# Transposing each own tile once, and scaling the copy by a row of ratios

## The chip, the cores and the metric

One core of a Trainium2 chip runs the whole program. TensorE (matrix products and transposes), VectorE, ScalarE and GpSimd compute, each working through its own list of instructions in order; SyncE issues the transfers. The engines wait for each other through semaphores. The metric is the device time of one execution in microseconds (us); lower is better.

## The reference

The input `x` is 8 sequences of 1024 tokens with 512 channels. Everything is float32.

```python
xn = layernorm(x, eps=1e-5)
out = x + attn(xn) + ffn(xn)
# attn: xs = xn shifted by one token
xm = xn * time_mix + xs * (1 - time_mix)
k = exp(min(xm @ Wk.T, 60)); v = xm @ Wv.T; r = xm @ Wr.T
# per head, a decaying running sum over the tokens
wkv, sum_k = decay_sum(k * v), decay_sum(k)
attn = (sigmoid(r) * wkv / sum_k) @ Wo.T
# ffn: a second layernorm (eps 1e-3), then a ternary product
y = layernorm(xn, eps=1e-3) * ln_gamma + ln_beta
g = max(abs(y)) over the whole input
ffn = clip(y * 128 / g) @ w_ternary * (g * beta / 128)
```

Both layernorms take mean and variance of the same token, so the second result is the first one times a number of that token. `g` is a maximum over all eight sequences, so no product of the second part can begin before all of `y` is known.

## The kernel before, in words

**Phases.** The eight sequences are worked off as batches 0 to 7, each in two tiles of 512 tokens (t = 0, 1). Phase A is batches 0 to 3: the attention part of the batch, and besides the second layernorm of that batch ("own") and of the batch four later ("other"), whose results go to memory while VectorE keeps their largest absolute value. Phase B is batches 4 to 7: the attention part again, and the ternary products of all eight batches.

**A batch** is 24 groups (g = 0 to 23). Group g is `project(g)` on TensorE, 12 products of 128x128 by 512 columns (float32 split into a high and a low part, three products for each of four channel blocks): k, v and r in turn for one 128-channel chunk c = g // 3. Chunks 0 to 3 belong to tile 0, chunks 4 to 7 to tile 1. After group 12 comes `attn_out` of tile 0, after group 23 that of tile 1: 48 products each, four chunks j by four banks by three. Chunk j is multiplied when VectorE has made its low part (`rwkv_lo`, L996); behind that stands a long chain on VectorE and ScalarE for every chunk: exp, k*v (L966), two scans (L976), a sum (L983), logarithm (L731), quotient (L736), product (L992), high part (L750) and low part.

**Slots.** In phase A each group also carries one slot: four transposes of 128x128 (L466) that bring one channel block of a normalised tile into a PSUM bank with the channels on the partitions. The order of the 24 slots is written out by hand: `ffn_own0` (slots 0 to 3), `ffn_other0` (4 to 7), `mix_own1` (8 to 11), `ffn_own1` (12 to 15), `ffn_other1` (16 to 19), `mix_next0` (20 to 23; the next batch's tile 0). Two banks take turns. ScalarE empties a slot (`evacuate`): a mix slot by two instructions (L616, L617) from which VectorE makes the mixed input (L898), ScalarE its high part (L662) and VectorE its low part (L922); an ffn slot by one (L625, scale gamma, bias beta), an "other" one by two (L624 keeps a plain copy). VectorE then takes the absolute maximum of an ffn slot (L905). TensorE's group 12 needs the four low parts of `mix_own1`, the next batch's group 0 those of `mix_next0`.

**Where the slots' tiles come from.** An own tile is normalised twice into the same buffer `normed`, once for the mix slots and once for the ffn slots: two of its four 128-token blocks by GpSimd (L1174), two by ScalarE (L677). The second waits until the transposes of the first have read the buffer. The scales are made on GpSimd by small instructions, after VectorE's statistics (L842; in groups 4, 12, 16 and at the batch's end).

**The start.** TensorE transposes four mix slots of batch 0 (`"P"`), while the weights are split into high parts (ScalarE for Wk and Wr, GpSimd for Wv and Wo) and low parts (VectorE, L927). ScalarE goes on to batch 0 when the low parts of Wr are done.

**Phase B** has no slots. The mix input is read back from memory, and GpSimd multiplies it by a row (L1247).

Of the kernel before, what the change touches and what calls it, by code (L numbers as in the profile page):

```python
# [22 lines left out]
F32 = mybir.dt.float32  # L23
# [5 lines left out]
P = 128  # L29
# [27 lines left out]

BANK_USES = {"A": ["attn0", "attn1"],
# [4 lines left out]
def mixed_decay_kernel(nc, x, constants, weights, Wf, out):  # L63
# [19 lines left out]
    with ExitStack() as ctx:  # L83
# [27 lines left out]
        AL = sb("ffn_lo", [P, CH, TILE], F32R)  # L111
        KV = sb("k_and_kv", [P, 2, 2, TILE])
# [18 lines left out]
        inv = sb("mix_over_ffn_stat", [P, 2, Q])  # L131
        gamb = sb("gamma_beta", [P, CH])
# [47 lines left out]
        act_c = sem("act_constants")  # L180

# [21 lines left out]
        pool_v = sem("pool_mix_input")  # L203

# [8 lines left out]
        STEPS, MIX_STEPS, OTHER_STEPS = 9, 3, 3  # L213
# [5 lines left out]
        def slots_before(b, ph, n):  # L219

            return n if ph == "P" else CH + len(SLOTS) * b + n

# [26 lines left out]
        def normed_count(b, ph, kind):  # L249

            if ph == "A":
                return 4 * b + [k for k in SLOT_KINDS if "other" not in k].index(kind) + 1
            return 4 * HALF + 2 * (b - HALF) + ["mix_own1", "mix_next0"].index(kind) + 1
# [36 lines left out]
        first_banks = [TB[:, :]] + [KVR[:, i, :] for i in range(3)]  # L290
# [16 lines left out]
        def _(sp):  # L307
# [35 lines left out]
            def batch_a(b, is_last=False):  # L343
                for n in range(7):
                    store_ffn_input(b, n)
                sp.wait_ge(pe_t, slots_before(b, "A", first_slot("ffn_other0") + CH))
# [12 lines left out]
                if not is_last:  # L359
                    sp.wait_ge(pe_t, slots_before(b, "A", first_slot("ffn_other1") + CH))  # L360
                    sp.dma_start(ZA[:, :, :], x_t[b + HALF + 1, 0]).then_inc(s_oth, 16)
                store_ffn_input(b, 19)
                store_row(b, 1)
                if is_last:
# [7 lines left out]
                    sp.wait_ge(pe_t, slots_before(b, "A", first_slot("ffn_other1") + CH))  # L372
                    for ch in range(CH):
                        sp.dma_start(ZA[:, ch, :], ffn_in[0, 0, ch]).then_inc(s_fld[ch], 16)
                    sp.wait_ge(pe_t, slots_before(b, "A", len(SLOTS)))
# [80 lines left out]
        def _(pe):  # L456
            pe.sem_inc(pe_g, CREDIT)
            pe.sem_inc(pe_rw, BANKS - 1)
# [18 lines left out]
            pe.wait_ge(dve_x, 2)  # L477

            def slot(b, ph, n):
                kind, ch = slot_of(ph, n)  # L480

                pe.wait_ge(act_u, slots_before(b, ph, n) - (n not in (0, ATTN0_AFTER + 1)))
                if n == 1:
                    pe.wait_ge(dve_out, BANKS + bank_use(b, ph, "attn0"))
                if n == ATTN0_AFTER + 2:
# [32 lines left out]
            def attn_out(b, ph, t):  # L518
# [3 lines left out]
                for j in range(CH):  # L522
                    pe.wait_ge(dve_rl, RING + CHUNKS * b + 4 * t + j + 1)
                    for q in range(Q):
                        if j == 0 and ph == "A":
                            pe.wait_ge(dve_out, first_bank + q + 1)
                            if q == Q - 1:
# [62 lines left out]
        def _(act):  # L590
# [3 lines left out]

            def evacuate(b, ph, n):
# [5 lines left out]
                if ph != "B":  # L601
                    act.wait_ge(pe_t, m + 1)
# [11 lines left out]
                elif mix:  # L614
                    if ph != "P":
                        nc.scalar.activation(U[:, r, :], bank, ACT.Copy, scale=tmx[:, ch:ch + 1])  # L616
                    nc.scalar.activation(shifted(ph, n), bank, ACT.Copy,  # L617
                                         scale=tmx1[:, ch:ch + 1]).then_inc(act_u, 1)
                elif ph == "A":
# [5 lines left out]
                    nc.scalar.activation(U[:, r, :], bank, ACT.Identity, bias=bet[:, ch:ch + 1],  # L625
# [38 lines left out]
            def normalise(b, ph, kind):  # L664
# [9 lines left out]
                i = 4 * b if kind == "ffn_own0" else stats_number(b, ph, tile)  # L674
                act.wait_ge(pool_step, STEPS + steps_before(i, ph) + (OTHER_STEPS if "other" in kind else STEPS if ffn else MIX_STEPS))
# [32 lines left out]
            act.wait_ge(pool_step, STEPS + STEPS)  # L708
            for q in ACT_CHUNKS:
                last = nc.scalar.activation(XN[:, q, :], X[0][:, q, :], ACT.Identity,  # L710
                                            bias=own[:, 0, 3, q:q + 1], scale=own[:, 0, 2, q:q + 1])
            last.then_inc(act_xn, 1)
            weight_hi("r")

# [583 lines left out]
```

## Time and profile before

| | |
|---|---|
| median of 3 runs | 892.61 us (891.09 to 892.99) |
| the profiled execution, its own time | 891.49 us |
| its span, first to last instruction | 889.7 us |
| TensorE busy (products) | 867.1 us, 97% of the span |
| VectorE | 764.8 us, 86% |
| ScalarE | 510.3 us, 57% |
| GpSimd | 215.2 us, 24% |
| granted clock of TensorE over the span | 1.000 |

In the profile PE is TensorE, PEld its weight loads, DVE VectorE, ACT ScalarE, POOL GpSimd; L12 is line 12 of the kernel. A timeline row reads: start and length in us, engine, line, operation, output<-input with partitions x elements, how many were merged, and in brackets the idle time before it and what ended it. TensorE's products are pipelined, so starts are compared, not lengths. In the view of busy time in stretches each row reads: the stretch, its length, then busy us (and instructions) of PE, PEld, DVE, ACT and POOL, the granted clock of TensorE, the share of time that the DMA engines worked, and GB/s. Batch 1 runs from 125.60 to 224.50.

### The profile page before, as it was taken

Reading aid. Unit: us, or ns where it says so; the run is one execution under the profiler, and the core shown is the slowest. Engines: PE = TensorE matmul, PEld = TensorE weight load, DVE = VectorE, ACT = ScalarE, POOL = GpSimd, SP = SyncE. Lnnn points to the kernel's source line nnn. Section 1 sums busy time; section 2 is a strip of 40 time slices with the busy share of each in tenths; the row PEclk is TensorE's granted clock in tenths of the full one; section 3 lists DMA queues with packets and bytes.
Section 4 is the critical chain, followed back from the end, with each engine's and each line's share of the span. In section 5 each row is a group of like instructions: output and inputs, shape, how many; then the busy total and the mean of one; then the engine's idle time right before and its main releaser. Section 6 shows DMA issues by size and latency. Waiting matters only on the chain.

```text
span 889.7 us, 12792 instructions
## 1 busy us (share of the span) xinstructions
PE 867.1 (97%) x3984; PEld 714.5 (80%) x3984; DVE 764.8 (86%) x1278; ACT 510.3 (57%) x834; POOL 215.2 (24%) x242
## 2 busy tenths in 40 slices
PE   3989999999999999999999999999999999999998
PEld 2778888888888888888888888888888888888886
DVE  5998999989897999989897897878978888789684
ACT  5584767667594757566564554545546536365441
POOL 5552326242452425240030100200201103011000
PEclk9999999999999999999999999999999999999999
DMA  8222415041423224045643245324451443424311
GB/s 283 108 83 88 149 54 184 13 171 54 165 71 135 101 82 154 12 172 136 212 145 115 84 154 189 125 75 141 153 175 57 157 141 96 154 93 142 95 48 47
DMA packets 59841, 107.13 MB, mean 120 GB/s; under 512 B 7712, under 2 KB 7712, under 8 KB 59808
## 3 DMA queue, kind: packets, MB, share of 16 engines
q1 hardware_dynamic: 59808, 106.73, 35.1%
q8 instruction: 16, 0.26, 0.1%
q14 instruction: 17, 0.14, 0.1%
HBM read 64.76 MB, written 41.96 MB: 120 GB/s over the span
## 4 chain that ended last, share of the span: by engine, by line
PE 90%; DVE 3%; issue 2%; POOL 2%; ACT 1%; DMA 0%; SPq 0%; POOLq 0%; DVEq 0%; ACTq 0%
PE kvr L513 18%; PE kvr L515 18%; PE kvr L514 18%; PE out_banks L552 7%; PE out_banks L554 7%; PE out_banks L534 6%; PE out_banks L533 6%; PE out_banks L531 6%; PE transposed L466 2%; PE out_banks L466 2%; DVE bn_stats L842 1%; POOL normed L1174 1%; POOL own_stats L1156 1%; POOL own_stats L1157 1%; DMA x<-in_x 0%
## 5 line engine op out<-in xcount | busy, mean ns | idle before, releaser
L1247 POOL TENSOR_TENSOR evacuated<-normed,mix_over_ffn_row 128x512 f32<-128x512 f32 x28 | 49.0, 1751 | 339.0 <-DVE ffn_lo L922 339.0
L513 PE MATMUL kvr<-xm_hi,wk_hi 128*128 128x512 f32 x256 | 103.7, 405 | 2.6 <-DVE xm_lo L922 2.6
L513 PE MATMUL kvr<-xm_hi,wv_hi 128*128 128x512 f32 x256 | 102.9, 402 | 2.2 <-DVE wv_lo L927 1.3
L513 PE MATMUL kvr<-xm_hi,wr_hi 128*128 128x512 f32 x256 | 102.7, 401 | 0.0
L515 PE MATMUL kvr<-xm_hi,wk_lo 128*128 128x512 f32 x256 | 101.0, 395 | 0.0
L514 PE MATMUL kvr<-xm_lo,wk_hi 128*128 128x512 f32 x256 | 100.7, 394 | 0.0
L515 PE MATMUL kvr<-xm_hi,wv_lo 128*128 128x512 f32 x256 | 100.2, 391 | 0.0
L515 PE MATMUL kvr<-xm_hi,wr_lo 128*128 128x512 f32 x256 | 100.1, 391 | 0.0
L531 PE MATMUL out_banks<-wo_hi,rwkv_hi 128*128 128x512 f32 x256 | 100.0, 390 | 0.0
L534 PE MATMUL out_banks<-wo_hi,rwkv_lo 128*128 128x512 f32 x256 | 99.7, 389 | 0.0
L514 PE MATMUL kvr<-xm_lo,wr_hi 128*128 128x512 f32 x256 | 99.7, 389 | 0.0
L514 PE MATMUL kvr<-xm_lo,wv_hi 128*128 128x512 f32 x256 | 99.7, 389 | 0.0
L552 PE MATMUL out_banks<-w_ternary,ffn_hi 128*128 128x512 f32 x256 | 99.6, 389 | 0.0
L533 PE MATMUL out_banks<-wo_lo,rwkv_hi 128*128 128x512 f32 x256 | 99.6, 389 | 0.0
L554 PE MATMUL out_banks<-w_ternary,ffn_lo 128*128 128x512 f32 x256 | 99.6, 389 | 0.0
L724 ACT ACTIVATE gate<-kvr 128x512 f32<-128x512 f32 x64 | 37.9, 593 | 90.7 <-PE kvr L515 90.7
L983 DVE SCALAR_TENSOR_TENSOR k_and_kv<-k_and_kv,constants,scans 128x1024 f32<-128x1024 f32 x64 | 83.3, 1302 | 1.1
L976 DVE TENSOR_TENSOR_SCAN scans<-constants,state,k_and_kv 128x512 f32<-128x512 f32 x64 | 79.7, 1286 | 0.0
L976 DVE TENSOR_TENSOR_SCAN scans<-constants,k_and_kv 128x512 f32<-128x512 f32 x64 | 75.8, 1226 | 0.0
L662 ACT ACTIVATE ffn_hi<-evacuated 128x512 fp32r<-128x512 f32 x64 | 39.9, 624 | 48.5 <-DVE evacuated L908 46.2
L1174 POOL TENSOR_SCALAR normed<-x,own_stats 128x512 f32<-128x512 f32 x34 | 55.0, 1623 | 51.2 <-PE out_banks L466 26.1
L922 DVE TENSOR_TENSOR ffn_lo<-evacuated,ffn_hi 128x512 fp32r<-128x512 f32 x64 | 43.9, 687 | 25.4 <-ACT ffn_hi L662 25.1
(140 smaller groups left out, 1922.7 us busy)
## 6 DMA issues: line engine op xcount, KB each, us to landing
other<-ffn_input SPq DMA_DIRECT2D x64, 256.0 KB, 5.1
x<-in_x SPq DMA_DIRECT2D x15, 1024.0 KB, 5.8
other<-in_x SPq DMA_DIRECT2D x8, 1024.0 KB, 5.8
ffn_input<-evacuated SPq DMA_DIRECT2D x32, 256.0 KB, 4.4
ffn_input<-parked SPq DMA_DIRECT2D x32, 256.0 KB, 2.2
attn_scratch<-x SPq DMA_DIRECT2D x8, 1024.0 KB, 4.2
parked<-attn_scratch SPq DMA_DIRECT2D x8, 1024.0 KB, 6.7
out<-parked SPq DMA_DIRECT2D x8, 1024.0 KB, 5.2
```

Of the source, the lines that this page charges most:

```text
L513: nc.tensor.matmul(KVR[:, m, :], hi, XH[t][:, ch, :], start=(ch == 0), stop=False)
L514: nc.tensor.matmul(KVR[:, m, :], hi, XL[t][:, ch, :], start=False, stop=False)
L515: last = nc.tensor.matmul(KVR[:, m, :], lo, XH[t][:, ch, :], start=False, stop=(ch == CH - 1))
L531: nc.tensor.matmul(OUT[:, q, :], hi, WH["o"][:, j, :], start=(j == 0 and ph == "A"), stop=False)
L533: nc.tensor.matmul(OUT[:, q, :], hi, WL["o"][:, j, :], start=False, stop=False)
L534: last = nc.tensor.matmul(OUT[:, q, :], lo, WH["o"][:, j, :], start=False, stop=(j == CH - 1))
L552: nc.tensor.matmul(OUT[:, q, :], AH[:, ch, q * P:(q + 1) * P], WQ[:, ch, :], start=(ch == 0), stop=False)
L554: last = nc.tensor.matmul(OUT[:, q, :], AL[:, ch, q * P:(q + 1) * P], WQ[:, ch, :], start=False, stop=(not own_tile and ch == CH - 1))
L976: last = V.tensor_tensor_scan(S[:, i, 1:TILE + 1], dec, kv[:, i, :], 0.0 if t == 0 else state[:, j, i:i + 1], ALU.mult, ALU.add)
L983: V.scalar_tensor_tensor(kv, kv, first[:, j:j + 1], S[:, :, 0:TILE], ALU.mult, ALU.add).then_inc(dve_sum, 1)
L1174: last = G.tensor_scalar(dst[:, q, :], src[:, q, :], stats[:, 2 * ffn, q:q + 1], stats[:, 2 * ffn + 1, q:q + 1], ALU.mult, ALU.add)
L1247: G.tensor_tensor(U[:, n % RING, :], XN[:, ch, :], BC[:, :], ALU.mult).then_inc(pool_v, 1)
```

## The change

An own tile is normalised once, for the mix slots. While ScalarE empties a mix slot it also copies the plain transposed block into a new buffer `Y`. The second layernorm of the same block is that copy times a row with one ratio for each token, `(var / (var + 1e-5) + 1e-3) ** -0.5`. GpSimd makes the ratios as columns (its last small steps fall away), TensorE turns each column, repeated 128 times, into a row that stands on all partitions (four transposes for a tile, into an output bank, after groups 9 and 21; the very first into the bank of the slots), ScalarE copies the row to SBUF, and GpSimd multiplies `Y` by it, one instruction of 128x512 for each block. The ffn slots of own tiles become virtual: ScalarE empties them from `Y` and TensorE has nothing to do for them. The "other" tiles and phase B stay as they are.

```diff
+        def is_virtual(n):
+            return SLOTS[n][0].startswith("ffn_own")
...
+ROW_AFTER = {9: 1, 21: 0}
...
     # TensorE
+            def ratio_row(k, t, bank):
+                pe.wait_ge(pool_ratio, k + 1)
+                for q in range(Q):
+                    last = nc.tensor.transpose(bank[:, q * P:(q + 1) * P],
+                                               ratio[:, t, q:q + 1].to_broadcast([P, P]), ident[:, :])
+                last.then_inc(pe_row, 1)
+
+            ratio_row(0, 0, TB)
...
-                    if ph == "B":
+                    if ph == "B" or n is not None and is_virtual(n):
                         n = None
...
+                    if ph == "A" and g in ROW_AFTER:
+                        t = ROW_AFTER[g]
+                        pe.wait_ge(dve_out, bank_use(b, ph, f"attn{1 - t}") + 1)
+                        ratio_row(2 * b + 2 - t, t, OUT[:, 0, :])
...
     # ScalarE
+            def copy_row(k, t, bank):
+                act.wait_ge(pe_row, 2 + k + 1)
+                nc.scalar.activation(RROW[:, t, :], bank, ACT.Copy).then_inc(act_row, 1)
...
+                if virtual:
+                    act.wait_ge(pool_z, virtual_before(b, n) + 1)
...
+                        nc.scalar.activation(Y[:, ch, :], bank, ACT.Copy)
                         nc.scalar.activation(U[:, r, :], bank, ACT.Copy, scale=tmx[:, ch:ch + 1])
...
-                    nc.scalar.activation(U[:, r, :], bank, ACT.Identity, bias=bet[:, ch:ch + 1],
+                    nc.scalar.activation(U[:, r, :], Y[:, ch, :] if virtual else bank, ACT.Identity,
...
+                    if ph == "A" and g - 1 in ROW_AFTER:
+                        t = ROW_AFTER[g - 1]
+                        copy_row(2 * b + 2 - t, t, OUT[:, 0, :])
                     if part1_first:
                         evacuate(b, ph, n)
...
-                                normalise(b, ph, "ffn_own1")
...
-                    normalise(b + 1, ph, "ffn_own0")
...
     # ScalarE in the start, after the high parts of Wr
+            for ch in range(CH):
+                last = nc.scalar.activation(Y[:, ch, :], first_banks[ch], ACT.Copy)
+            copy_row(0, 0, TB[:, :])
...
     # GpSimd
-                pool.wait_ge(pe_t, slots_before(b, "A", first_slot("mix_own1") + CH))
-                normalise(XN, X[1], own[:, 1], 1, pool_xn)
+                for ch in range(CH):
+                    own_ffn_input(b, first_slot("ffn_own1") + ch)
                 other(b, "other1")
...
-                    normalise(XN, X[0], own[:, 0], 1, pool_xn)
+                    for ch in range(CH):
+                        own_ffn_input(b + 1, first_slot("ffn_own0") + ch)
                     other(b + 1, "other0")
+
+            def own_ffn_input(b, n):
+                kind, ch = SLOTS[n]
+                t = int(kind[-1])
+                pool.wait_ge(act_row, 2 * b + t + 1)
...
+                G.tensor_tensor(Y[:, ch, :], Y[:, ch, :], RROW[:, t, :], ALU.mult).then_inc(pool_z, 1)
```

In the start GpSimd's four multiplies for batch 0 stand between its casts of Wo and its work on the first "other" tile. TensorE's waits for free slot banks are counted over the slots that are left.

## Rows read from the trace of the kernel before

**Rows 1.** Busy time in two stretches: a batch of phase A, one of B.

```profile
125.60:224.50 98.90, 98.80 (x482) 81.37 (x481) 90.39 (x159) 66.28 (x108) 39.24 (x48) 1.00 0.31 107
...
530.00:649.00 119.00, 119.00 (x526) 98.54 (x525) 99.06 (x157) 60.04 (x98) 14.64 (x8) 1.00 0.38 128
```

**Rows 2.** The same view: groups 0 to 3 and 8 to 11, batch 1.

```profile
125.60:138.40 12.80, 12.80 (x66) 10.56 (x65) 11.54 (x23) 6.22 (x9) 7.30 (x9) 1.00 0.63 224
...
151.30:164.30 13.00, 13.00 (x65) 10.84 (x66) 12.86 (x25) 11.66 (x21) 5.55 (x8) 1.00 0.23 81
```

**Rows 3.** Timeline of TensorE: slots 9 and 10 of batch 1.

```profile
154.54 0.60 PE L466 MATMUL out_banks<-ident,normed 128*128 128x128 f32 x4
...
157.74 0.60 PE L466 MATMUL transposed<-ident,normed 128*128 128x128 f32 x4
```

**Rows 4.** The same in phase B: first products of two groups in a row.

```profile
427.48 0.39 PE L513 MATMUL kvr<-xm_hi,wr_hi 128*128 128x512 f32 x1
...
430.19 0.39 PE L513 MATMUL kvr<-xm_hi,wk_hi 128*128 128x512 f32 x1
```

**Rows 5.** Timeline of all engines: slot 8 of batch 1.

```profile
148.28 2.95 POOL L1174 TENSOR_SCALAR normed<-x,own_stats 128x512 f32<-128x512 f32 x2 [0.39 <-POOL own_stats L1157]
...
151.29 0.66 PE L466 MATMUL transposed<-ident,normed 128*128 128x128 f32 x4
```

**Rows 6.** Timeline of ScalarE in batch 1.

```profile
139.55 0.59 ACT L624 ACTIVATE parked<-transposed 128x512 f32<-128x512 f32 x1
140.03 0.78 ACT L625 ACTIVATE evacuated<-transposed,constants 128x512 f32<-128x512 f32 x1
...
163.92 0.64 ACT L662 ACTIVATE xm_hi<-evacuated 128x512 fp32r<-128x512 f32 x1
...
216.35 0.72 ACT L731 ACTIVATE k_and_kv<-k_and_kv,k_eps 128x512 f32<-128x512 f32 x1 [0.93 <-DVE k_and_kv L983]
```

**Rows 7.** Timeline of VectorE in batch 1.

```profile
161.21 1.29 DVE L922 TENSOR_TENSOR xm_lo<-evacuated,xm_hi 128x512 fp32r<-128x512 f32 x2
...
163.72 1.71 DVE L922 TENSOR_TENSOR xm_lo<-evacuated,xm_hi 128x512 fp32r<-128x512 f32 x2
...
173.89 0.69 DVE L996 TENSOR_TENSOR rwkv_lo<-k_and_kv,rwkv_hi 128x512 fp32r<-128x512 f32 x1 [0.70 <-ACT rwkv_hi L750]
...
219.89 0.69 DVE L996 TENSOR_TENSOR rwkv_lo<-k_and_kv,rwkv_hi 128x512 fp32r<-128x512 f32 x1
```

**Rows 8.** Timeline of TensorE: end of group 12, last chunks of both outputs.

```profile
166.17 0.39 PE L513 MATMUL kvr<-xm_hi,wk_hi 128*128 128x512 f32 x1
...
175.49 0.39 PE L531 MATMUL out_banks<-wo_hi,rwkv_hi 128*128 128x512 f32 x1
...
221.57 0.39 PE L531 MATMUL out_banks<-wo_hi,rwkv_hi 128*128 128x512 f32 x1
```

**Rows 9.** View of line 1247: min/median/max in ns, first and last start.

```profile
L1247 POOL TENSOR_TENSOR evacuated<-normed,mix_over_ffn_row x28: 1288/1297/3455, 446.9 to 808.5; 128x512 f32<-128x512 f32 x28
```

**Rows 10.** Timeline of all engines in phase B around one GpSimd multiply.

```profile
517.14 0.74 DVE L890 SCALAR_TENSOR_TENSOR evacuated<-evacuated,constants,shifted_part 128x511 f32<-128x511 f32 x1
...
518.56 1.30 POOL L1247 TENSOR_TENSOR evacuated<-normed,mix_over_ffn_row 128x512 f32<-128x512 f32 x1 [7.03 <-DVE ffn_lo L922]
...
518.59 1.82 DVE L890 SCALAR_TENSOR_TENSOR evacuated<-evacuated,constants,shifted_part 128x511 f32<-128x511 f32 x1
```

**Rows 11.** Timeline of VectorE in the start.

```profile
21.91 4.15 DVE L927 TENSOR_TENSOR wv_lo<-x,wv_hi 128x512 fp32r<-128x512 f32 x4
...
25.98 2.48 DVE L927 TENSOR_TENSOR wr_lo<-k_and_kv,wr_hi 128x512 fp32r<-128x512 f32 x4
...
35.20 0.67 DVE L966 TENSOR_TENSOR k_and_kv<-k_and_kv,kvr 128x512 f32<-128x512 f32 x1
```

**Rows 12.** Waits of TensorE: total us, times, longest; first and last.

```profile
PE transposed L466 <- POOL normed L1174: 14.3, 2, 12.1
...
PE kvr L513 <- DVE k_and_kv L966: 0.9, 1, 0.9
```

More of the change, by code:

```diff
@@ L56 @@
 RING = 4
+FFN_ROOM = 176640
+ROW_AFTER = {9: 1, 21: 0}
 BANK_USES = {"A": ["attn0", "attn1"],
@@ L180, in mixed_decay_kernel @@
         act_c = sem("act_constants")
+        act_first = sem("act_first_own_copied")
+        act_row = sem("act_ratio_row_copied")
+        pe_row = sem("pe_ratio_row")
         dve_c = sem("dve_constants")
@@ L203, in mixed_decay_kernel @@
         pool_v = sem("pool_mix_input")
+        pool_ratio = sem("pool_ratio_row")
+        pool_z = sem("pool_own_ffn_input")
         dve_past = sem("dve_past_wait")
@@ L221, in slots_before, with pe_slots_before, virtual_before @@
             return n if ph == "P" else CH + len(SLOTS) * b + n
+        def is_virtual(n):
+            return SLOTS[n][0].startswith("ffn_own")
+        def pe_slots_before(b, ph, n):
+            if ph == "P":
+                return n
+            per_batch = sum(not is_virtual(k) for k in range(len(SLOTS)))
+            return CH + per_batch * b + sum(not is_virtual(k) for k in range(n))
+        def virtual_before(b, n):
+            return 2 * CH * b + sum(is_virtual(k) for k in range(n))
         def ffn_stores_before(b, n):
@@ L251, in normed_count @@
             if ph == "A":
-                return 4 * b + [k for k in SLOT_KINDS if "other" not in k].index(kind) + 1
-            return 4 * HALF + 2 * (b - HALF) + ["mix_own1", "mix_next0"].index(kind) + 1
+                return 2 * b + ["mix_own1", "mix_next0"].index(kind) + 1
+            return 2 * HALF
         def stats_number(b, ph, tile):
@@ L288, in shifted @@
             return E[:, n % 2, :] if ph == "P" and n > 1 else WS[:, n % 2, :]
-        first_banks = [TB[:, :]] + [KVR[:, i, :] for i in range(3)]
+        first_banks = [OUT[:, q, :] for q in range(Q)]
         def slot_bank(ph, n):
@@ L457, in _ @@
             pe.sem_inc(pe_g, CREDIT)
+            pe.sem_inc(pe_row, 2)
             pe.sem_inc(pe_rw, BANKS - 1)
@@ L526, in attn_out @@
                             pe.wait_ge(dve_out, first_bank + q + 1)
+                            if q == 0:
+                                pe.wait_ge(act_row, 2 * b + 2 + t)
                             if q == Q - 1:
@@ L600, in evacuate @@
                 mix = kind.startswith("mix")
-                if ph != "B":
-                    act.wait_ge(pe_t, m + 1)
+                virtual = ph == "A" and is_virtual(n)
+                if virtual:
+                    act.wait_ge(pool_z, virtual_before(b, n) + 1)
+                elif ph != "B":
+                    act.wait_ge(pe_t, pe_slots_before(b, ph, n) + 1)
                 act.wait_ge(dve_lo, m + 1)
@@ L672, in normalise @@
                 ffn = kind.startswith("ffn")
-                i = 4 * b if kind == "ffn_own0" else stats_number(b, ph, tile)
-                act.wait_ge(pool_step, STEPS + steps_before(i, ph) + (OTHER_STEPS if "other" in kind else STEPS if ffn else MIX_STEPS))
+                i = stats_number(b, ph, tile)
+                act.wait_ge(pool_step, STEPS + steps_before(i, ph) + (OTHER_STEPS if "other" in kind else MIX_STEPS))
                 for q in ACT_CHUNKS:
@@ L707, in _ @@
                 high_part(0, "P", m)
[L708 to L712, printed above, removed]
             weight_hi("r")
+            for ch in range(CH):
+                last = nc.scalar.activation(Y[:, ch, :], first_banks[ch], ACT.Copy)
+            last.then_inc(act_first, 1)
+            copy_row(0, 0, TB[:, :])
             act.wait_ge(dve_w, 3 * CH)
@@ L1005, in add_out @@
                     for normed in (pool_xn, act_xn):
-                        dve.wait_ge(normed, CREDIT + (4 * HALF if ph == "B" else normed_count(b, ph, f"ffn_own{t}")))
+                        dve.wait_ge(normed, CREDIT + (2 * HALF if ph == "B" else 2 * b + t))
                     if ph == "B":
@@ L1181, in _ @@
             normalise(XN, X[0], own[:, 0], 0, pool_xn)
-            ffn_scale(0, 0, own[:, 0])
-            pool.wait_ge(pe_t, CH)
-            normalise(XN, X[0], own[:, 0], 1, pool_xn)
+            ffn_scale(0, 0, own[:, 0], 0, 0)
             pool.wait_ge(s_w[1], 16)
@@ L1252, in batch_b @@
                         mix_input(b, n)
+            for ch in range(CH):
+                own_ffn_input(0, first_slot("ffn_own0") + ch)
             other(0, "other0")
```

47 lines of the change are left out of this document (26 added, 21 removed).

## The prediction

> **What bounds the kernel now.** I read the busy time in stretches first, to see which engine sets each stage [rows 1]. In a batch of phase A (125.60 to 224.50) TensorE is busy 98.80 of 98.90 us, in a batch of phase B 119.00 of 119.00: TensorE sets the time, and the list of its waits [rows 12] is short: the longest entry is 14.3 us, 12.1 of them the wait for the first normalised tile. So a transpose taken off TensorE is worth its time, as long as nobody else becomes late. The second view is who is next. VectorE is busy 90.39 us of that batch, but not evenly: over groups 8 to 11 it has 12.86 of 13.00 us, and ScalarE 11.66 of 13.00 [rows 2], while in groups 0 to 3 VectorE has 1.26 us free and ScalarE 6.58. The third view is the timeline around the points where TensorE reads what VectorE wrote last; there I read margins.
>
> **What is removed, and what a slot is worth.** Two neighbouring slots of the mix tile start 3.20 us apart (157.74 - 154.54) with the twelve matmuls of one group between them [rows 3]. In phase B the same twelve without a slot take 2.71 us (430.19 - 427.48) [rows 4]. A slot of four transposes costs TensorE 0.49 us. Per batch eight slots go and two rows of four transposes come. A row's transposes have the same shape as a slot's, but read one column repeated, which no row shows; bounds are nothing (a load of repeated values could be cheaper) and twice a slot, 0.98. I take 0.49, since the form and the output are those of rows 3. So TensorE gains 8 x 0.49 - 2 x 0.49 = 2.94 us a batch. In batch 0 slots 0 to 3 are worth nothing: TensorE there waits in any case for VectorE's k*v of chunk 0 (0.9 us [rows 12], ending at 35.87 [rows 11]) and would only wait longer. Batch 0 gains 0.98. The ceiling is 3 x 2.94 + 0.98 = 9.8 us. The ninth row lies in the start, where TensorE has idle time.
>
> **Does the gain of groups 0 to 3 survive to group 8?** Slot 8 was started by GpSimd's normalise (148.28 + 2.95 = 151.23, TensorE at 151.29 [rows 5]), so that chain had no margin. Its head is the statistics behind slot 4, and slot 4 comes as much earlier as four slots are worth; VectorE has 1.26 us free in groups 0 to 3 and what it waits for there is TensorE's. I let the whole 1.96 through. The steps that the new row needs are small ones of four columns right behind that normalise, and the row stands two groups later, 6.4 us by rows 3: no wait.
>
> **Place 1, groups 8 to 13.** ScalarE gets four copies of the mix tile and a row copy ahead of the high part of slot 11. A copy from PSUM occupies it 0.48 us (140.03 - 139.55 [rows 6]): 2.4 us. It had 1.34 us free there [rows 2]; I let it absorb 1.0, as part of its idle time is too early. The high part moves from 163.92 to about 165.3 (bounds: 1.06 and 2.4 late). The last low part then ends near 166.6 instead of 163.72 + 1.71 = 165.43 [rows 6, 7]. TensorE wants it at 166.17 [rows 8], 0.49 later because of the row: just met. But behind it VectorE has the whole recurrence of chunk 3, and its rwkv_lo ended at 173.89 + 0.69 = 174.58 against TensorE's 175.49 [rows 7, 8]: margin 0.91, less 1.2: 0.3 us of stall. (The removed normalise of ScalarE stood behind the high part, so it gives nothing back to this chain; the row and the missing slot 12 cancel on TensorE.)
>
> To this come GpSimd's four multiplies, 1.30 us each where undisturbed (median of 28, up to 3.46) [rows 9], which must pass VectorE in its fullest stretch. Rows 10 show the price of a collision: the same instruction of 511 columns takes 0.74 us alone and 1.82 beside a multiply, 1.08 more. The two chunks of the normalise that now go cost VectorE 0.42 (1.71 against 1.29 for two low parts [rows 7]). Bounds for four multiplies: nothing (all in instructions or gaps that don't mind) and 4 x 1.08 - 0.42 = 3.9 us. I take 1.7: one fits where VectorE now waits for ScalarE, one in k*v from PSUM or the absmax, two collide. Stall at place 1: 0.3 + 1.7 = 2.0 us a batch (0.3 to 4.2).
>
> The Trainium skill ("SBUF — State Buffer", "Who interferes with whom") has the rule against this change: a VectorE instruction with two SBUF inputs and a GpSimd instruction that reads SBUF exclude each other for a whole instruction. The trace agrees in kind: 1.08 of 1.30 us [rows 10]. By the rule's full 1.30 the same share of collisions would cost, as an estimate, 0.22 us more each, some four a batch: 3.5 us more than my sum in all.
>
> **Place 2, groups 20 to 23 and the second output.** Three ScalarE copies (the row, two of the mix tile; those for slots 20 and 21 fall into its idle time) add 1.44 us ahead of the logarithm of chunk 7, which had waited 0.93 [rows 6]: 0.5 late. VectorE's last rwkv_lo ended at 219.89 + 0.69 = 220.58, TensorE reads at 221.57 [rows 7, 8]; with the row's 0.49 the margin is 1.48, less 0.5: 1.0. Four multiplies again, of which I let two collide (2.2) less the normalise taken away (0.42): 1.7 - 1.0 = 0.7 us (0 to 2.9). They must be done by the next batch's slot 0, over 10 us later: no wait.
>
> **The start.** ScalarE's copies and the row copy follow the casts of Wr, so the four multiplies become possible at about 25.7, when VectorE begins its four low parts of Wr (2.48 us [rows 11]). Four casts of GpSimd beside the low parts of Wv cost VectorE 4.15 - 2.48 = 1.67 us [rows 11]; four multiplies cost between nothing and 4 x 1.08 = 4.3. I take 2.5, the 1.67 drawn out by the longer instruction. All that VectorE does up to k*v of chunk 0 moves with it, and TensorE waits for that: + 2.5 us.
>
> **The sum.** Batches 1 to 3: 3 x (-2.94 + 2.0 + 0.7) = -0.7. Batch 0: -0.98 + 2.7 = +1.7. Start +2.5. Together +3.5 us, slower. The profiled execution took 891.49 us (span 889.7 and 1.8 around it), so 895.0 by its own time; it lies 1.1 below the median of the three runs, 892.61, and against that I predict 896.0. Nothing else moves: phase B, SyncE's order of transfers and the VectorE work per slot are the same.
>
> **Rivals.** With s for the stall of a batch, the change is 2.5 + 4s - 9.8.
> 1. *Slower, as summed* (s = 2.7): VectorE, already full in groups 8 to 13, is pushed by ScalarE and GpSimd past TensorE. For it: 0.14 us free in 13.00 [rows 2], margins under 1 us. From s = 2.3 it is over 0.2% slower. 896.
> 2. *Faster*: GpSimd's multiplies wait until VectorE does statistics, absmax or sums out of PSUM, and cost it nothing; only ScalarE's lateness stays. s = 0.5 and 1.0 at the start: 1.0 + 2.0 - 9.8 = -6.8, 886. It decides for s below about 1.4. For it: two normalise chunks in the fullest stretch cost VectorE only 0.42 [rows 7], and the median multiply ran undisturbed [rows 9]. Against: the multiply holds on longer, and rows 10.
> 3. *Break-even*: s between 1.4 and 2.3, within 1.8 us (0.2%, about what a measurement can tell from no change). 893.
> 4. *A new wait*: the first multiply of a tile is starved; ScalarE's evacuation of slot 12 stands ahead of exp, logarithm and quotient of chunks 3 and 4, so all of them wait. The longest multiply was 3.46 us, 2.2 over the median [rows 9]; once a batch on top of place 1: +8.6 on the sum, 905. Against: ScalarE reaches that slot two groups after the row copy. The Trainium skill ("SBUF — State Buffer", the same section) lets the instruction issued first go first; a VectorE that is back to back would then keep GpSimd out, which is this case. No row of phase A has a multiply.
> 5. *The row costs twice a slot*: 8 x 0.49 = +3.9 on any of these; I see no sign of it and count it inside their spread.
>
> **How the numbers follow.** Chances: slower as summed 0.42, faster 0.31, break-even 0.20, new wait 0.07. So faster 0.31, same 0.20, slower 0.49. The extreme ends of the bounds (s = 0.3 with no cost at the start, -8.6; s = 7.1 with 4.3, +23) are unlikely to meet. The range leaves out a tenth on each side: 886 to 904; the likeliest case's own is 894.5 to 902.
>
> **What the profile afterwards would show.** Right: 32 multiplies of 128x512 on GpSimd in phase A, 92 fewer transposes (128 out, 36 in); a pitch between batches of 98 to 100 us; TensorE idle ahead of the first product of group 12 or of the output product, released by low parts or rwkv_lo, 1 to 3 us a batch; VectorE instructions of two SBUF inputs lengthened by about 1 us beside multiplies; k*v of chunk 0 near 38. Wrong: a batch pitch near 96 with no such idle time (rival 2), or ScalarE waiting for GpSimd at slot 12 (rival 4).

## The result, and the profile after

The change takes 917.61 us (median of 4, 916.51 to 917.84) against 892.43 us (median of 4, 891.09 to 892.99): ratio 1.0282, 95% interval 1.0264 to 1.0300. It is slower, as forecast, but by 25 us where 3.5 were forecast, far outside the range of 886 to 904. The profiled execution has a span of 914.2 us against 889.7. The prediction named a pitch between batches of 98 to 100 us as its sign; batch 1 now takes 104.8 us, 98.9 before.

The page first: busy time of each engine, and the engines' shares of the chain that ended last.

```profile
PE 867.5 (95%) x3892; PEld 709.4 (78%) x3892; DVE 791.5 (87%) x1278; ACT 521.3 (57%) x863; POOL 242.8 (27%) x246
...
PE 60%; DVE 19%; issue 10%; ACT 4%; POOL 3%; DMA 3%; DVEq 0%; ACTq 0%; SPq 0%; POOLq 0%
```

VectorE has as many instructions as before (1278) and is busy 26.7 us longer (791.5 against 764.8). So it has no more work; its instructions have become longer. TensorE's list of waits, which answers to [rows 12]:

```profile
PE kvr L556 <- DVE xm_lo L979: 12.3, 11, 2.0
PE out_banks L576 <- DVE rwkv_lo L1053: 6.4, 3, 2.1
PE kvr L556 <- DVE wr_lo L984: 3.7, 1, 3.7
```

These three lie at the three places of the prediction: place 1 (group 12; 2.6 of the 12.3 us belong to the start, as before), place 2 (the second output) and the start. Timelines of place 1 in batch 1, GpSimd, VectorE, then TensorE, to be held against [rows 7, 8]:

```profile
169.45 7.14 POOL L1306 TENSOR_TENSOR own_normed<-own_normed,ffn_over_mix_rows 128x512 f32<-128x512 f32 x4 [5.43 <-ACT ffn_over_mix_rows L647]
...
171.97 3.49 DVE L979 TENSOR_TENSOR xm_lo<-evacuated,xm_hi 128x512 fp32r<-128x512 f32 x2
175.38 1.76 DVE L1049 TENSOR_TENSOR k_and_kv<-k_and_kv,gate 128x512 f32<-128x512 f32 x1
...
178.47 0.50 PE L556 MATMUL kvr<-xm_hi,wk_hi 128*128 128x512 f32 x1 [1.99 <-DVE xm_lo L979]
```

Two low parts take 3.49 us instead of 1.29 beside the multiplies, a product 1.76 instead of 0.69: three instructions of VectorE are lengthened by about 1.1 us each at four multiplies. TensorE stands for 1.99 us ahead of the third quarter of group 12. Place 2 in the same batch:

```profile
224.39 6.89 POOL L1306 TENSOR_TENSOR own_normed<-own_normed,ffn_over_mix_rows 128x512 f32<-128x512 f32 x4 [8.56 <-ACT ffn_over_mix_rows L647]
...
216.94 2.45 DVE L1033 TENSOR_TENSOR_SCAN scans<-constants,state,k_and_kv 128x512 f32<-128x512 f32 x2
...
224.39 0.68 DVE L1023 TENSOR_TENSOR k_and_kv<-k_and_kv,kvr 128x512 f32<-128x512 f32 x1
224.98 0.73 DVE L1028 COPY scans<-state 128x2 f32<-128x2 f32 x1
225.63 4.56 DVE L1033 TENSOR_TENSOR_SCAN scans<-constants,state,k_and_kv 128x512 f32<-128x512 f32 x2
230.23 2.13 DVE L1040 SCALAR_TENSOR_TENSOR k_and_kv<-k_and_kv,constants,scans 128x1024 f32<-128x1024 f32 x1
...
234.50 0.50 PE L576 MATMUL out_banks<-wo_hi,rwkv_hi 128*128 128x512 f32 x1 [2.14 <-DVE rwkv_lo L1053]
```

The two scans of the chunk before took 2.45 us (at 216.94, no multiply beside them), here 4.56; the sum takes 2.13 instead of 1.28. Together 2.96 us, again for three of four multiplies: the first lay beside k*v out of PSUM, which took 0.68 us as ever. The copy of 128x2 behind it took 0.73 us instead of 0.16, so 3.5 us in all. The gap of TensorE stands ahead of the third of the output's four chunks. The prediction read its margin ahead of the fourth (0.99 us [rows 7, 8]); ahead of the third it was 217.71 + 0.68 against 218.85 in the kernel before, 0.46 us:

```profile
217.71 0.68 DVE L996 TENSOR_TENSOR rwkv_lo<-k_and_kv,rwkv_hi 128x512 fp32r<-128x512 f32 x1
...
218.85 0.39 PE L531 MATMUL out_banks<-wo_hi,rwkv_hi 128*128 128x512 f32 x1
```

Behind the 2.14 us gap TensorE is slow for a while. Busy time in three stretches, from that gap's end on (columns as in [rows 1], granted clock third from the end):

```profile
234.50:235.50 1.00, 1.00 (x4) 0.86 (x5) 0.96 (x2) 0.24 (x2) 0.00 (x0) 1.00 0.00 0
235.50:238.90 3.40, 3.40 (x9) 2.64 (x8) 3.27 (x8) 1.95 (x4) 0.00 (x0) 0.50 0.00 0
238.90:241.60 2.70, 2.70 (x13) 2.21 (x12) 2.09 (x4) 0.46 (x1) 0.00 (x0) 0.99 0.00 0
```

At 0.50 (1.2 instead of 2.4 GHz) a product takes 0.43 us, not 0.23: 24 products from 234.50 on last 7.19 us to the next group, 1.7 longer than at full clock.

In the start, VectorE's four low parts of Wr stand beside the first four multiplies, and all four are lengthened (2.48 us in [rows 11]):

```profile
25.59 6.81 DVE L984 TENSOR_TENSOR wr_lo<-k_and_kv,wr_hi 128x512 fp32r<-128x512 f32 x4
```

The view of line 1306 has all 32 multiplies (min/median/max in ns, first and last start):

```profile
L1306 POOL TENSOR_TENSOR own_normed<-own_normed,ffn_over_mix_rows x32: 1294/1744/2219, 25.5 to 383.5; 128x512 f32<-128x512 f32 x32
```

One by one in the trace, 7 of them took 1.29 to 1.34 us and 25 took 1.70 to 2.22. The lengthened VectorE instructions of some size are 25 as well: 4 in the start, 12 at place 1, 9 at place 2, by 0.85 to 1.1 us each.

The ledger by groups is worked out from the starts of the first products of each group: pitch after less pitch before, in us, batches 0 to 3. A slot that is gone is worth -0.35 to -0.49 in it.

| kernel | group 12 (place 1) | group 23 (place 2) |
|---|---|---|
| the change | +3.86 +2.63 +3.79 +2.61 | +3.67 +3.69 +2.07 0.00 |
| no multiplies | -0.17 -0.13 -0.14 -0.14 | -0.36 -0.36 -0.35 0.00 |
| `Y` filled, not multiplied | -0.19 -0.17 -0.17 -0.17 | -0.36 -0.37 -0.35 0.00 |
| no copies on ScalarE | +1.92 +3.83 +2.65 +3.61 | +3.69 +2.08 +3.72 0.00 |
| multiplies of place 2 and start moved | +1.85 +3.87 +2.55 +3.81 | -0.35 -0.37 -0.35 -0.01 |
| all multiplies moved | -0.24 -0.19 -0.22 -0.24 | -0.36 -0.36 -0.35 0.00 |

In batch 3 the change itself has no multiplies at place 2 (there is no next batch in phase A), but the row and ScalarE's copy for it: 0.00. At place 1 the batches of the change differ by the clock alone: ahead of the third quarter of group 12 TensorE stands for 1.98 to 2.00 us in all four; the clock falls in 0 and 2 (+3.8) and stays at 1.00 in 1 and 3 (+2.6). But the 1.2 us of that fall are not lost for good. From the first product of group 12 to slot 20, 39.2 to 39.3 us pass in all four batches: those without a fall wait 1.05 us at slot 20 for the next batch's tile, those with one don't.

### The profile page after: what moved, and what is told of

The parts are those of the page before. It is cut to its first block, busy times and chain, and to the rows that moved or that the text cites. A ratio compares the mean times of both kernels' runs of the same rounds, so it can differ in the third digit from the quotient of the medians.

```text
span 914.2 us, 12688 instructions
## 1 busy us (share of the span) xinstructions
PE 867.5 (95%) x3892; PEld 709.4 (78%) x3892; DVE 791.5 (87%) x1278; ACT 521.3 (57%) x863; POOL 242.8 (27%) x246
## 4 chain that ended last, share of the span: by engine, by line
PE 60%; DVE 19%; issue 10%; ACT 4%; POOL 3%; DMA 3%; DVEq 0%; ACTq 0%; SPq 0%; POOLq 0%
PE kvr L556 11%; PE kvr L558 11%; PE kvr L557 11%; PE out_banks L597 6%; PE out_banks L599 6%; PE out_banks L576 5%; PE out_banks L578 5%; PE out_banks L579 5%; DVE scans L1033 4%; DVE bn_stats L899 3%; DVE x L1071 1%; DVE xm_lo L979 1%; DVE k_and_kv L1049 1%; POOL normed L1233 1%; DVE k_and_kv L1023 1%
## 5 line engine op out<-in xcount | busy, mean ns | idle before, releaser
L1316 POOL TENSOR_TENSOR evacuated<-normed,mix_over_ffn_row 128x512 f32<-128x512 f32 x28 | 51.3, 1831 | 336.8 <-DVE ffn_lo L979 336.8
L556 PE MATMUL kvr<-xm_hi,wk_hi 128*128 128x512 f32 x256 | 103.2, 403 | 12.3 <-DVE xm_lo L979 12.3
L576 PE MATMUL out_banks<-wo_hi,rwkv_hi 128*128 128x512 f32 x256 | 102.4, 400 | 6.5 <-DVE rwkv_lo L1053 6.4
L578 PE MATMUL out_banks<-wo_lo,rwkv_hi 128*128 128x512 f32 x256 | 101.7, 397 | 0.0
L1040 DVE SCALAR_TENSOR_TENSOR k_and_kv<-k_and_kv,constants,scans 128x1024 f32<-128x1024 f32 x64 | 85.9, 1342 | 1.1
L1033 DVE TENSOR_TENSOR_SCAN scans<-constants,state,k_and_kv 128x512 f32<-128x512 f32 x64 | 84.8, 1367 | 0.0
L808 ACT ACTIVATE rwkv_hi<-k_and_kv 128x512 fp32r<-128x512 f32 x64 | 40.3, 630 | 55.5 <-DVE k_and_kv L1049 55.5
L556 PEld LDWEIGHTS kvr<-xm_hi,wk_hi 128*128 128x128 f32 x256 | 48.3, 189 | 27.1 <-DVE xm_lo L979 16.0
L1306 POOL TENSOR_TENSOR own_normed<-own_normed,ffn_over_mix_rows 128x512 f32<-128x512 f32 x32 | 55.7, 1771 | 47.7 <-ACT ffn_over_mix_rows L647 47.7
```

Source lines behind the costliest of these rows:

```text
L556: nc.tensor.matmul(KVR[:, m, :], hi, XH[t][:, ch, :], start=(ch == 0), stop=False)
L576: nc.tensor.matmul(OUT[:, q, :], hi, WH["o"][:, j, :], start=(j == 0 and ph == "A"), stop=False)
L578: nc.tensor.matmul(OUT[:, q, :], hi, WL["o"][:, j, :], start=False, stop=False)
L1033: last = V.tensor_tensor_scan(S[:, i, 1:TILE + 1], dec, kv[:, i, :], 0.0 if t == 0 else state[:, j, i:i + 1], ALU.mult, ALU.add)
L1040: V.scalar_tensor_tensor(kv, kv, first[:, j:j + 1], S[:, :, 0:TILE], ALU.mult, ALU.add).then_inc(dve_sum, 1)
L1306: G.tensor_tensor(Y[:, ch, :], Y[:, ch, :], RROW[:, t, :], ALU.mult).then_inc(pool_z, 1)
```

## Experiments

**What blocks VectorE.** First the multiplies were left out, then ScalarE's copies, then each multiply was replaced by a fill of the same block.

```diff
 # no multiplies (GpSimd does nothing to Y; ScalarE waits for its own copy)
-                for ch in range(CH):
-                    own_ffn_input(b, first_slot("ffn_own1") + ch)
...
 # no copies
-                        nc.scalar.activation(Y[:, ch, :], bank, ACT.Copy)
...
 # fills
-                G.tensor_tensor(Y[:, ch, :], Y[:, ch, :], RROW[:, t, :], ALU.mult).then_inc(pool_z, 1)
+                G.memset(Y[:, ch, :], 1.0).then_inc(pool_z, 1)
```

> The multiplies are left out: ScalarE empties the virtual slots from the copy as it is, so the second layernorm lacks its ratio. All else stays, ScalarE's copies and the rows of ratios too. Theory 1 (the multiplies hold up VectorE's instructions of two SBUF inputs, and TensorE waits for VectorE): 884 to 889, that is 3 to 8 us under the kernel before, since the eight slots taken off TensorE then count and only the lateness of ScalarE's copies is left. Theory 2 (ScalarE's copies make the chains late): 905 or more. Theory 3 (the rows of ratios on TensorE and their waits in order): 905 or more.

Measured: 891.68 us, 0.9989 of before (0.9980 to 0.9999). 26 us come back, and both stalls are gone (table). But 884 to 889 was expected: nearly all of TensorE's gain is still missing. That question is taken up below.

> ScalarE's copy of each mix slot into the new buffer is left out (the multiplies work on what is in the buffer); rows and multiplies stay. Theory 1: 912 to 917, little under the changed kernel, for the multiplies are all there. Theory 2: 889 to 895. Theory 3: 913 to 918.

Measured: 915.83 us, 1.0248 (1.0225 to 1.0272). Theory 1 as to the 25 us; theory 2 falls. Theory 3 would give the same time here, but it fell with the kernel without multiplies, which keeps the rows and their waits.

> Each multiply becomes a fill of the same 128x512 block with ones: GpSimd writes SBUF but reads none. Theory 1 in the form that what GpSimd reads is what blocks VectorE: 884 to 890, as without multiplies. Theory 1 in the form that any GpSimd work on SBUF blocks VectorE: in between, 895 to 912, by the length of the fills. Theories 2 and 3: 910 to 918.

Measured: 891.39 us, 0.9988 (0.9978 to 0.9999), as without multiplies. Fills of 0.53 us (median) at the same places cost VectorE 0.1 us in all. Busy time of the engines, without multiplies and with fills:

```profile
PE 860.4 (97%) x3892; PEld 705.6 (79%) x3892; DVE 761.4 (86%) x1278; ACT 520.2 (59%) x863; POOL 189.8 (21%) x214
```

```profile
PE 861.0 (97%) x3892; PEld 706.3 (79%) x3892; DVE 761.5 (86%) x1278; ACT 519.8 (58%) x863; POOL 206.8 (23%) x246
```

VectorE is busy 761.4 and 761.5 us against 791.5 with the change: 30.1 us for 32 multiplies, 0.94 us each, on average over all of them. GpSimd's multiplies take 1771 ns on average, where they take 1300 when nothing is in the way (below): each side waits for the other. They take turns: where they collide VectorE has no pause, and still each multiply comes in after one instruction of VectorE. The Trainium skill ("SBUF — State Buffer", "Who interferes with whom") says that a VectorE instruction with two SBUF inputs contends with a GpSimd instruction that reads SBUF, not with one that only writes it; the trace agrees on both halves.

A fourth kernel let GpSimd read one input, the row, instead of two.

```diff
+                G.tensor_copy(Y[:, ch, :], RROW[:, t, :]).then_inc(pool_z, 1)
```

> Each multiply becomes a copy of the row of ratios into the block: GpSimd reads one input instead of two, for 0.6 to 1.0 us instead of 1.30, at the same places (the second layernorm is replaced by the row). Theory 1, blocked by what GpSimd reads, for as long as it reads: 896 to 908, between no multiplies and the change. If only two inputs on both sides block: 890 to 893, as with the fills.

Measured: 893.23 us, 1.0011 (1.0001 to 1.0021): below the expected range of theory 1 and just above that of its rival. The lines view has the copies at 963 ns on average (607 at the least), and the page has VectorE at 769.2 us:

```profile
L1307 POOL COPY own_normed<-ffn_over_mix_rows 128x512 f32<-128x512 f32 x32 | 30.1, 963 | 64.2 <-ACT ffn_over_mix_rows L647 50.0 <-ACT shifted_part L675 10.7 <-issue 1.9
```

So a reading copy does block, 7.8 / 32 = 0.24 us each, but a microsecond for four of them is within the margins of both places (group 12 -0.06 to -0.02, group 23 -0.34 to 0.00). What was wrong was to scale the time with the blocked time: below the margin it is almost free.

**The same multiplies beside other work.** The next batch's four wait for the last low part of the batch, those of the start for the low parts of Wr.

```diff
+                    pool.wait_ge(dve_lo, RING + slots_before(b, "A", len(SLOTS)))
                     for ch in range(CH):
                         own_ffn_input(b + 1, first_slot("ffn_own0") + ch)
...
+            pool.wait_ge(dve_w, 3 * CH)
             for ch in range(CH):
                 own_ffn_input(0, first_slot("ffn_own0") + ch)
```

> Complete computation. The four multiplies for the next batch's first tile wait until VectorE has made the last low part of the batch, so that they lie beside its sums out of PSUM and its statistics; the four of the start wait for the last low part of Wr. The four of the other tile stay where they are. Theory 1: the stall ahead of the last chunk of the second output goes in batches 0 to 2 (pitch of group 23 3.67, 3.69 and 2.07 longer than before, now within 0.3 of it), so 9 us less, and the start gives 2 us back: 905 to 909. Theories 2 and 3: 914 to 918, unchanged.

Measured: 906.85 us, 1.0143 (1.0126 to 1.0160). Place 2 is clean. The time lies in the expected range with one of its two terms missing, partly by luck: the three stalls at place 2 were 10.5 us (against the kernel without multiplies) where 9 were expected, and the start gave nothing back. Its timeline shows side by side what is blocked and what not:

```profile
28.07 2.46 DVE L899 BATCH_NORM_STATS2 bn_stats<-other 128x6 f32<-128x512 f32 x4
...
30.96 4.67 DVE L984 TENSOR_TENSOR wo_lo<-parked,wo_hi 128x512 fp32r<-128x512 f32 x4
...
28.42 6.06 POOL L1308 TENSOR_TENSOR own_normed<-own_normed,ffn_over_mix_rows 128x512 f32<-128x512 f32 x4 [2.62 <-DVE wr_lo L984]
```

The statistics (one input) take 2.46 us beside the first multiplies, as they take alone; four low parts (two inputs) take 4.67 beside the later ones instead of 2.47.

Then all of them were moved: the other tile's behind the low part of chunk 3, with ScalarE's evacuation and VectorE's maximum of slot 12 behind them, and in the start two behind the low parts of Wr, two behind those of Wo.

```diff
+                pool.wait_ge(dve_rl, RING + CHUNKS * b + CH)
                 for ch in range(CH):
                     own_ffn_input(b, first_slot("ffn_own1") + ch)
```

> Complete computation, all 32 multiplies, each beside work of VectorE that doesn't have two SBUF inputs. Besides what was moved before: the four of the other tile wait for the low part of chunk 3, so that they lie beside the statistics and the sums of the first output (ScalarE's evacuation and VectorE's maximum of slot 12 move behind them); of the four in the start two lie beside the statistics, two wait until the low parts of Wo are made. Theory 1: 891 to 895, what the kernel without multiplies takes, plus 0 to 3 for the start; pitch of group 12 back to within 0.5 of before. A rival within it, that a multiply costs its time wherever it stands (GpSimd and VectorE share more than the second input): 906 to 918, as 32 x 1.0 would still be paid somewhere.

Measured: 896.37 us, 1.0044 (1.0029 to 1.0058). With the same 32 multiplies 21 of the 25 us are gone; the rival that a multiply costs its time anywhere falls. Timelines of GpSimd and VectorE in batch 1, four multiplies beside statistics and sums out of PSUM:

```profile
180.30 5.06 POOL L1316 TENSOR_TENSOR own_normed<-own_normed,ffn_over_mix_rows 128x512 f32<-128x512 f32 x4 [21.83 <-DVE rwkv_lo L1056]
...
179.95 2.46 DVE L902 BATCH_NORM_STATS2 bn_stats<-other 128x6 f32<-128x512 f32 x4
...
182.87 2.48 DVE L1074 TENSOR_TENSOR x<-x,out_banks 128x512 f32<-128x512 f32 x4
```

Neither side is lengthened (1.27 us a multiply). VectorE's busy time is 762.5 us. One of the 32 still collided, in the start, with an instruction that has a single SBUF input; the same takes 0.42 us alone:

```profile
33.30 1.32 DVE L1018 TENSOR_SCALAR k_and_kv<-k_and_kv 128x512 f32<-128x512 f32 x1
```

**Where TensorE's gain goes.** Without multiplies 9.8 us were still to be gained, and 1.0 came. The ledger of that kernel has a loss of 1.1 to 1.4 us in group 19 of every batch (the pitch that holds slot 20) and of 0.4 to 0.5 in group 3 (slot 4) of batches 1 to 3. Its timelines, VectorE, SyncE (SPq is its issue of a transfer) and TensorE in batch 1:

```profile
177.69 2.48 DVE L1074 TENSOR_TENSOR x<-x,out_banks 128x512 f32<-128x512 f32 x4
...
180.20 0.37 SPq L385 DMA_DIRECT2D attn_scratch<-x  x1
...
184.46 0.38 SPq L388 DMA_DIRECT2D x<-in_x  x1
...
190.41 2.47 DVE L902 BATCH_NORM_STATS2 bn_stats<-x 128x6 f32<-128x512 f32 x4 [1.17 <-DMA x<-in_x]
...
199.91 0.66 PE L499 MATMUL out_banks<-ident,normed 128*128 128x128 f32 x4 [0.98 <-POOL normed L1236]
```

The sums of the first output end at 180.17, are stored, the next batch's tile is loaded into the same buffer, and VectorE, idle for it, begins the statistics at 190.41: 10.2 us that don't get shorter when three slots leave groups 13 to 15. In the expectations below, theory 4 is that this way holds TensorE up at slot 20, theory 5 that ScalarE's copies use up the rest of the gain. The first try was to take slot 20 behind the products of group 20, with and without multiplies.

```diff
-                    late = g == ATTN0_AFTER or (is_first and g < 2 * CH)
+                    late = g == ATTN0_AFTER or (is_first and g < 2 * CH) or (ph == "A" and g == 20)
```

> No multiplies (the second layernorm lacks its ratio), and slot 20 behind the products of group 20. Theory 4: 4 to 5 us under the kernel without multiplies, 886 to 888, and no wait of TensorE at slot 20 left. Theory 5: 890 to 893.

Measured: 891.58 us, 0.9983 (0.9973 to 0.9993). The wait at slot 20 is gone (group 19 now -0.35 to -0.44), but group 20 is 0.3 longer and group 23 is +0.74 to +0.91 instead of -0.36: with slot 20 later, TensorE waits 0.6 to 1.0 us for rwkv_lo at the third chunk of the second output. That this comes by way of ScalarE's chain was not tested.

> Complete computation: as the kernel with all multiplies moved, and TensorE takes slot 20 behind the products of group 20 instead of ahead of them. Theory 4 (what the multiplies leave of the gain goes into a wait for the next batch's tile, which comes from memory no earlier than before, 1.2 to 1.4 us at slot 20 in each batch): 4 to 5 us under the kernel with slot 20 in its place, so 886 to 891. Theory 5 (the copies on ScalarE use up the rest): no difference within 1 us.

Measured: 896.38 us, 1.0049 (1.0032 to 1.0065): no difference, theory 4 in this form brings nothing. With all multiplies moved there was little left to gain at slot 20: group 19 loses 0.1 to 0.4 there, because a new wait of 0.9 us at slot 16 stands ahead of it. The second try shortens the way itself, by quarters.

```diff
-                sp.wait_ge(dve_out, BANKS + bank_use(b, "A", "attn0") + Q)
-                sp.dma_start(scratch_t[b, 0], X[0][:, :, :]).then_inc(s_xst[0], 16)
-                store_ffn_input(b, 13)
-                sp.wait_ge(s_xst[0], 16 * b + 16)
-                sp.dma_start(X[0][:, :, :], x_t[b + 1, 0]).then_inc(s_x[0], 16)
+                for q in range(Q):
+                    sp.wait_ge(dve_out, BANKS + bank_use(b, "A", "attn0") + q + 1)
+                    sp.dma_start(scratch_t[b, 0][:, q, :], X[0][:, q, :]).then_inc(s_xsq[q], 16)
+                for q in range(Q):
+                    sp.wait_ge(s_xsq[q], 16 * b + 16)
+                    sp.dma_start(X[0][:, q, :], x_t[b + 1, 0][:, q, :]).then_inc(s_x[0], 16)
+                store_ffn_input(b, 13)
```

> No multiplies (the second layernorm lacks its ratio), and the first tile's way through memory by quarters. Theory 4 in its second form: 886 to 888.5, no wait of TensorE at slot 20. If the wait only moves on: 891 to 892.

Measured: 885.82 us, 0.9924 (0.9911 to 0.9938). The loss in group 19 is gone (-0.06 to 0.00), and 5.0 us with it by the two profiles (5.9 between the medians): theory 4 in its second form.

> No multiplies and no copy of the mix slots on ScalarE either (the second layernorm is made from what is in the buffer). Theory 5 (ScalarE's copies use up what the multiplies leave of the gain): 885 to 889. Theory 4: 891 to 892, as with the copies.

Measured: 886.65 us, 0.9929 (0.9913 to 0.9944), so theory 5 holds as well, at other places: group 19 still loses 0.84 to 1.10, but group 12 is -0.84 to -0.87 instead of -0.13 to -0.17, and group 3 -0.13 in batches 1 and 2 instead of +0.5. ScalarE's copies cost 0.7 us at place 1 and 0.65 at slot 4. Each of the two takes about half of the gain; both edits together weren't tried. The kernel before with the quarters alone is the control:

> The kernel before, with the first tile's way through memory by quarters and nothing else. Theory 4 (the wait for that way appears only when slots 12 to 15 leave TensorE): 892 to 893, no change. If the kernel before waited for it as well: 887 to 889.

Measured: 893.36 us, 1.0008 (0.9997 to 1.0019): it didn't wait for that way.

**A version faster than both.** With all multiplies moved the start still cost 3.5 us up to slot 8 of batch 0 (55.80 against 52.31), and slot 16 had its new wait of 0.9 us. First only GpSimd's order in the start was changed (two multiplies, the normalise of the other tile, two multiplies).

> Complete computation: as the kernel with all multiplies moved, but in the start GpSimd makes two of the four multiplies only after its normalise of the first other tile, for which TensorE waited 2.56 us in that kernel. Theory 1: the 4.3 us that the start still cost shrink to 1 to 2.5: 893 to 895. If the start's loss is not GpSimd's order: 896 again.

Measured: 894.90 us, 1.0024 (1.0014 to 1.0035). With the quarters besides:

> Complete computation: as the kernel with the start mended, and the first tile's way through memory (sums of the first output stored, the next batch's tile loaded into the same buffer) goes by quarters instead of as a whole, ahead of the stores of slots 13 to 15. Theory 4 in its second form (the gain is lost because this way takes 10.0 us, 180.2 to 190.4 in the kernel without multiplies, and TensorE's shorter groups 13 to 15 don't shorten it): the wait at slot 20 goes, 3 to 5 us less: 888 to 892. If it only moves on, as with slot 20 put later: as before this edit within 1 us.

Measured: 892.13 us, 1.0004 (0.9993 to 1.0014): just above the range. Group 19 loses nothing any more, but it had lost only 0.0 to 0.25 us ahead of this edit. Of the 3.1 us between the two profiles 1.6 are a fall of the clock in group 8 of batch 0 and 1.3 the group 3 of batches 1 to 3; that slot 20 is the reason isn't shown by this run. Then VectorE took over two of four multiplies in the start and at the other tile (0.68 us each, one instruction of its own instead of a collision).

```diff
+                                    for ch in (2, 3):
+                                        V.tensor_tensor(Y[:, ch, :], Y[:, ch, :], RROW[:, 1, :],
+                                                        ALU.mult).then_inc(dve_z, 1)
```

> Complete computation: as the kernel with the first tile's way by quarters, but of each four multiplies of the start and of the other tile VectorE makes two itself (0.7 us each, at places where TensorE doesn't wait for it), so that GpSimd is done when it is wanted for the first and second other tile. Theory 6 (what is still lost is GpSimd's own time: its multiplies make its next normalise late, 1.05 us at slot 16 of each batch and 2 to 3 in the start): 886 to 888.5. If what is lost lies in VectorE's or ScalarE's order: 891 to 893.

Measured: 888.67 us, 0.9959 of before (0.9944 to 0.9975), so 0.4% faster than the kernel before. Theory 6: the start's loss at slot 8 of batch 0 falls from 3.43 us to 0.47 (the kernel ahead of that has the same start and lost 2.70, so 0.7 us is scatter), and group 15, the pitch with slot 16, from +0.92 to -0.12. Group 19 loses 0.3 to 0.4 again, since VectorE's two multiplies stand ahead of its statistics. This kernel leaves nothing out.

## Why the prediction was wrong

- **Direction and mechanism: right.** The multiplies push VectorE past TensorE at the three places named; the rows named for it appeared.
- **What a slot and a row are worth: right.** Slots that leave show as -0.47 to -0.49 in the ledger, rows as +0.42 to +0.46 (forecast 0.49). The transposes of a repeated column cost what others cost, so rival 5 falls.
- **The share of multiplies that collide: the step that failed.** "one fits where VectorE now waits for ScalarE, one in k*v from PSUM or the absmax, two collide" at place 1, "of which I let two collide" at place 2, 2.5 of 4.3 us in the start. The price of a collision was right (forecast 1.08 us [rows 10], measured 0.85 to 1.1). But 25 of the 32 multiplies lengthened an instruction of VectorE: three of each four at places 1 and 2, all four in the start. The one beside k*v out of PSUM was seen rightly. The multiplies follow each other without a break for 7 us, and in such a stretch VectorE has almost nothing but two inputs from SBUF. In the start VectorE lost 6.81 - 2.48 = 4.33 us (2.5 taken, bound 4.3), and TensorE reaches slot 8 of batch 0 4.27 us later than without multiplies (56.26 against 51.99). At place 1 the stall beyond the kernel without multiplies is 2.75 us where the clock stayed (1.7 taken).
- **The margin at place 2: read at the wrong chunk.** 1.0 us was taken, ahead of the fourth chunk. TensorE came to stand ahead of the third, where the kernel before had 0.46. The stall is 2.4 us where the clock stayed (0.7 taken, bound 2.9).
- **The clock: missing from the sum, but most of it isn't lost.** The fall to 0.50 added 1.2 us at place 1 in two batches, 1.6 at place 2 in two, and 2.0 in the start (group 2 is 2.00 longer, 12 products at 0.43 us): 7.6 us on the spot. At place 1 it is gone again at slot 20 (above). In the start it adds nothing to slot 8, which follows VectorE's statistics, and VectorE is busy for 20.62 of the 20.79 us ahead of them. At place 2, 0.7 to 1.2 us a fall are left at the next batch's slot 8: from group 20 to the group behind that slot 52.2 us pass with a fall (batches 0 and 1) and 51.5 without (batch 2), and without multiplies the same stretch is 0.5 us shorter in batches 0 and 1. So about 2 of the 25 us are the clock's.
- **The ceiling of 9.8 us: wrong as a gain.** "I let the whole 1.96 through" was right only as far as slot 4, and no step looked at slot 20. Without multiplies batches 1 and 2 gain 0.5 to 0.7 us each instead of 2.94. The change itself meets that wait as well, 1.05 us at slot 20 in batches 1 and 3.
- **ScalarE's lateness at place 1: right in kind, mis-sized.** Forecast 0.3 us of stall; 0.7 measured by leaving the copies out.
- **Place 2 was counted in four batches**; the last has no multiplies there.
- **A wait of batch 0 was put to the wrong chunk.** The 0.9 us of [rows 12] stand at 46.75 and end with k*v of chunk 1, not with that of chunk 0. What follows from it, that slots 0 to 3 of batch 0 gain nothing, holds all the same.

The terms of the sum, and what the ledgers have for them up to the end of phase A. Place 1 goes up to slot 20, place 2 up to the next batch's slot 8:

| term | forecast | measured |
|---|---|---|
| transposes off TensorE, ScalarE's lateness (no multiplies) | -9.8 + 1.2 | -1.0 |
| the start, up to slot 8 | +2.5 | +4.3 |
| multiplies at place 1, four batches | +6.8 | +11.0 |
| multiplies at place 2 | +2.8 | +9.9 |
| sum | +3.5 | +24.2 |

Rival 4, a starved multiply, didn't happen: the longest took 2.22 us.

## What to carry to other kernels

In these runs a GpSimd instruction that reads SBUF was free beside VectorE's statistics, sums out of PSUM and maxima, and cost about a microsecond beside an instruction with two inputs from SBUF. List what VectorE does in those very microseconds, and count every overlap with a two-input instruction at a full collision. Compare the delay with the margin ahead of the bounding engine, at every chunk that it waits for and not only at the last: below the margin it costs almost nothing. Above it, ask whether what the clock takes after the stall would have been waited away further on. Work taken off the bounding engine pays only as far as the next fixed latency (here a tile's way through memory): follow each shortened stretch to what feeds its end.

## What the runs showed of the hardware

- **The same gap, with and without a fall of the clock.** Ahead of slot 8 of batch 0 TensorE stands for 2.10 to 2.15 us in all sixteen kernels, for the same reason. In eight, as without multiplies, the clock stays at 1.00 behind it; in the other eight, as without multiplies and copies, it falls to about 0.5 for some 3.5 us, and group 8 is up to 1.6 us longer (1.57 in that kernel). The stretches, first the one kernel, then the other:

```profile
53.00:56.70 3.70, 3.70 (x20) 3.04 (x19) 3.60 (x6) 3.67 (x7) 1.65 (x2) 1.00 0.60 200
```

```profile
53.10:56.60 3.50, 3.50 (x10) 2.63 (x9) 3.40 (x6) 1.84 (x4) 1.45 (x1) 0.51 0.63 212
```

What decides it stays open: the gap's length does not. Differences of 1.6 us between two profiles can be this alone.
- **A collision lengthens both sides**: over all 32 multiplies VectorE loses 0.94 us and GpSimd 0.47 (1771 against 1300 ns) for each, together a little more than its own length.
- **A single SBUF input is not always safe.** VectorE's copy of 128x2 (L1028) took 0.73 us instead of 0.16 beside a multiply, three times of three, and 0.50 beside a fill; the TENSOR_SCALAR above took 1.32 instead of 0.42 once.
- **A copy of one input on GpSimd blocks too**, 0.24 us on average, and grows itself from 0.61 to 0.96 us.
